# Experts of a routed feed-forward layer: 71 tiles in place of 72, with the last turns of the loops written out

## The reference

```
def _L1_ffn_ref(x, router_w, w_gate, w_up, w_down):   # x: 4096 tokens of 128, 8 experts, hidden 512, top 2
    scores = jax.nn.softmax(xf @ router_w.T, axis=-1)
    topk_scores, topk_ids = jax.lax.top_k(scores, TOP_K)
    topk_scores = topk_scores / topk_scores.sum(-1, keepdims=True)
    cw = (jax.nn.one_hot(topk_ids, N_EXPERTS, dtype=xf.dtype) * topk_scores[..., None]).sum(1)
    def body(acc, inputs):
        wg, wu, wd, w = inputs
        h = jax.nn.silu(xf @ wg) * (xf @ wu)
        return (acc + w[:, None] * (h @ wd), None)
# in the whole: x = x + 0.5 * _L1_ffn_ref(_layernorm(x), ...)
```

## Time and profile before

| | |
|---|---|
| median of three runs | 1526.19 us (1525.87 to 1528.49) |
| the profiled execution | 1528.99 us |
| its span, first to last instruction | 1527.3 us |
| mean granted TensorE clock | 0.876 |
| busy: PE, DVE, ACT, POOL | 76%, 65%, 52%, 39% of the span |
| instructions on all engines | 34396 |
| the first routed layer's tiles | about 680 to 886 us |
| the second routed layer's tiles | about 1290 to 1497 us |

### The profile page before, as it was taken

How to read it: one execution, slowest core, us unless ns; L and a number is a source line. 1 busy time by engine, 2 the same in 40 slices (tenths; PEclk the granted TensorE clock), 3 DMA queues, 4 the chain that set the end, 5 groups by cost and what they waited for, 6 DMA issues and landing times.

```text
span 1527.3 us, 34396 instructions
## 1 busy us (share of the span) xinstructions
PE 1166.0 (76%) x11393; PEld 901.6 (59%) x11394; DVE 997.7 (65%) x1974; ACT 787.2 (52%) x1333; POOL 592.1 (39%) x859
## 2 busy tenths in 40 slices
PE   0577559999984776549999914899998654999991
PEld 0355336666652555539999912455554353999991
DVE  5799769898955998573333356888997357333333
ACT  0444216555663443236666661567666523666666
POOL 2122122121200222016676723566766301667671
PEclk9999659999997998559999966899999855999996
DMA  8000023322210000101111133343243010111115
GB/s 255 19 1 0 1 49 58 53 55 55 51 24 1 1 0 1 55 9 46 47 48 46 47 123 56 58 78 65 56 83 58 2 56 9 46 47 48 47 47 178
DMA packets 161960, 75.58 MB, mean 49 GB/s; under 512 B 126540, under 2 KB 153941, under 8 KB 161877
## 3 DMA queue, kind: packets, MB, share of 16 engines
q1 hardware_dynamic: 152404, 55.06, 16.4%
q0 software_dynamic: 9472, 19.42, 4.3%
HBM read 28.69 MB, written 15.86 MB: 29 GB/s over the span
## 4 chain that ended last, share of the span: by engine, by line
PE 53%; DVE 24%; issue 7%; ACT 6%; DMA 3%; POOL 3%; SPq 2%; DVEq 1%; POOLq 0%; ACTq 0%
PE PS L990 17%; PE PS L1010 8%; PE PS L656 4%; PE PS L358 3%; DVE sg L790 2%; PE PS L638 2%; PE PS L622 2%; PE PS L575 2%; DVE m L790 2%; PE PS L950 2%; PE PS L610 1%; ACT pt L1070 1%; SPq L882 1%; DVE q_amax L266 1%; DMA qT<-qs 1%
## 5 line engine op out<-in xcount | busy, mean ns | idle before, releaser
L990 PE MATMUL PS<-xTs,pt 128*128 128x128 f32 x2336 | 287.7, 277 | 0.0
L715 ACT ACTIVATE pt<-PS 128x768 f32<-128x768 f32 (+1 forms) x256 | 227.6, 917 | 111.2 <-PE PS L638 59.4
L990 PEld LDWEIGHTS PS<-xTs,pt 128*128 128x128 f32 x2336 | 276.0, 194 | 0.0
L1114 DVE TENSOR_TENSOR pt<-pt,PS 128x512 f32<-128x512 f32 x146 | 100.4, 687 | 240.4 <-PE PS L990 210.9
L1227 POOL DMA_INDIRECT xs<-rows,src x152 | 147.3, 969 | 193.3 <-DVE src L1108 147.6
L1039 ACT ACTIVATE pt<-wgu 128x1024 f32 x148 | 156.2, 1057 | 93.2 <-issue 84.2
L1236 POOL DMA_INDIRECT outs<-ys,dst x144 | 142.0, 986 | 85.6 <-DVE ys L1122 78.5
L790 DVE TENSOR_REDUCE m<-PS 128x4 f32<-128x1024 f32 x128 | 149.2, 1217 | 12.9 <-PE PS L575 12.3
L1010 PE MATMUL PS<-wdn,pt 128*128 x1152 | 152.2, 275 | 0.0
L1010 PEld LDWEIGHTS PS<-wdn,pt 128*128 128x128 f32 x1152 | 140.0, 192 | 0.0
L575 PE MATMUL PS<-tables 64*128 64x128 bf16 (+2 forms) x1536 | 132.0, 251 | 0.0
(11 more groups left out here) (228 smaller groups left out, 2120.2 us busy)
## 6 DMA issues: line engine op xcount, KB each, us to landing
pt<-outs SPq DMA_DIRECT2D x16, 512.0 KB, 5.0
rows<-qT SPq DMA_DIRECT2D x12, 256.0 KB, 2.4
xs<-rows,src POOLq DMA_INDIRECT x152, 2.5
outs<-ys,dst POOLq DMA_INDIRECT x144, 2.3
wgu<-in_L_ffn_w_gate SPq DMA_DIRECT2D x1, 2048.0 KB
wgu<-in_L_ffn_w_up SPq DMA_DIRECT2D x1, 2048.0 KB
wdn<-in_L_ffn_w_down SPq DMA_DIRECT2D x8, 256.0 KB
qT<-hqT SPq DMA_DIRECT2D x128, 4.0 KB
```

Of the source, the lines that this page charges most:

```text
L715: s.activation(k.pt[:, a % 4, :, 0:w], k.PS[:, self.bank:self.bank + 2, 0:w], ACT.Exp, scale=self.scale).then_inc(self.s_p, 1)
L990: last = t.matmul(k.PS[:, 1 + 2 * p + w, c * P:(c + 1) * P], k.wst[:, 1 - p, w, c * P:(c + 1) * P], k.xTs[:, p, :], start=True, stop=True)
L1114: v.tensor_tensor(k.hs[:, p, :], k.sgs[:, p, :], k.PS[:, 2 + 2 * p, :], ALU.mult).then_inc(self.s_h, 1)
```

## The change

NS is 71, NL equals NS, and nothing is prepared for tiles beyond the last. Since 71 is divisible by neither 24 nor 4, the bodies of PE's, ACT's and DVE's loops became functions `tiles(m)`: with a loop variable they write a whole body, with a Python number they write only the tiles that exist (`has`). PE's loop now has 2 passes (48 tiles), and 23 tiles stand written out behind it. ACT's loop has 17 passes, with what is left of tiles 69 and 70 behind it. DVE's loop also ends after tile 67, with three tiles behind it. POOL gathers 71 times. The semaphores' final counts now differ over the four ring buffers (`self.turns`, `self.t0`).

```diff
@@ -42,11 +42,11 @@
 GT = 4
 NG = NT // GT
 RING = 4
-NS = 72
+NS = 71
 UN = 24
 TABLES = P + 2 * P + 3 * 384
-NL = NS + RING
-assert NS % UN == 0 and UN % RING == 0 and NS >= (2 * NT * P + NE * (P - 1)) // P
+NL = NS
+assert UN % RING == 0 and NS >= (2 * NT * P + NE * (P - 1)) // P
 CR = 2
 ROUND = 1.5 * 2.0 ** 23
 
@@ -926,7 +926,8 @@
         self.s_stored = k.sem(name + "_stored")
         self.s_scaled = k.sem(name + "_scaled")
 
-        self.ld0, self.st0 = run * 16 * (NS // RING + 1), run * 16 * (NS // RING)
+        self.turns = [len(range(u, NS, RING)) for u in range(RING)]
+        self.t0 = [run * 16 * n for n in self.turns]
         self.ga0 = run * 16 * (NG // RING)
         self.s_ld = [k.sem(f"moe_loaded_{i}") for i in range(RING)]
         self.s_st = [k.sem(f"moe_stored_{i}") for i in range(RING)]
@@ -974,7 +975,7 @@
             return t.value_load(k.eid[0:1, ds(n, 1)], min_val=0, max_val=NE - 1)
 
         def xT(n, r, before, back):
-            eng.wait_ge(self.s_ld[r], self.ld0 + 16 * before + 16)
+            eng.wait_ge(self.s_ld[r], self.t0[r] + 16 * before + 16)
             if back:
                 eng.wait_ge(self.s_xT, n - 1)
             t.transpose(k.PS[:, 7 * (r % 2), 0:P], k.xs[:, r, 0:D], k.ident[:, :]).then_inc(self.s_xT_ps, 1)
@@ -996,14 +997,22 @@
         xT(1, 1, 0, False)
         up(0, 0, 0)
         up(0, 0, 1)
-        with eng.Fori(0, NS // UN) as m:
+
+        def has(n):
+            return not isinstance(n, int) or n < NS
+
+        def tiles(m):
             e = expert(UN * m)
             for u in range(UN):
                 i, p = UN * m + u, u % 2
-                up(i + 1, 1 - p, 0)
-                up(i + 1, 1 - p, 1)
-                xT(i + 2, (u + 2) % RING, UN // RING * m + (u + 2) // RING, True)
-                e1 = expert(i + 1) if u + 1 < UN else None
+                if not has(i):
+                    break
+                if has(i + 1):
+                    up(i + 1, 1 - p, 0)
+                    up(i + 1, 1 - p, 1)
+                if has(i + 2):
+                    xT(i + 2, (u + 2) % RING, UN // RING * m + (u + 2) // RING, True)
+                e1 = expert(i + 1) if u + 1 < UN and has(i + 1) else None
                 eng.wait_ge(self.s_h, i + 1 + CR)
                 eng.wait_ge(self.s_y, i + CR)
                 for c in range(FC):
@@ -1011,6 +1020,9 @@
                                     start=c == 0, stop=c == FC - 1)
                 last.then_inc(self.s_y_ps, 1)
                 e = e1
+        with eng.Fori(0, NS // UN) as m:
+            tiles(m)
+        tiles(NS // UN)
 
     def scalar(self, eng):
         k, s = self.k, self.k.nc.scalar
@@ -1055,12 +1067,22 @@
         xT(0, 0, False)
         xT(1, 1, False)
         silu(0, 0)
-        with eng.Fori(0, NS // RING) as m:
+
+        def has(n):
+            return not isinstance(n, int) or n < NS
+
+        def tiles(m):
             for u in range(RING):
                 i, p = RING * m + u, u % 2
-                weights(i + 2, p, True)
-                silu(i + 1, 1 - p)
-                xT(i + 2, p, True)
+                if has(i + 2):
+                    weights(i + 2, p, True)
+                if has(i + 1):
+                    silu(i + 1, 1 - p)
+                if has(i + 2):
+                    xT(i + 2, p, True)
+        with eng.Fori(0, NS // RING) as m:
+            tiles(m)
+        tiles(NS // RING)
 
         for g in range(NG):
             eng.wait_ge(self.s_ga[g % RING], self.ga0 + 16 * (g // RING) + 16)
@@ -1112,18 +1134,26 @@
             eng.wait_ge(self.s_up_ps, n + 1)
             eng.wait_ge(self.s_y_ps, n - 1 + CR)
             v.tensor_tensor(k.hs[:, p, :], k.sgs[:, p, :], k.PS[:, 2 + 2 * p, :], ALU.mult).then_inc(self.s_h, 1)
+
+        def has(n):
+            return not isinstance(n, int) or n < NS
+
         def tiles(m):
             for u in range(RING):
                 i, p = RING * m + u, u % 2
-                h(i + 1, 1 - p)
+                if not has(i):
+                    break
+                if has(i + 1):
+                    h(i + 1, 1 - p)
                 eng.wait_ge(self.s_y_ps, i + 1 + CR)
-                if not isinstance(m, int) or self.run:
-                    eng.wait_ge(self.s_st[u], self.st0 + 16 * m)
+                if not isinstance(m, int) or m or self.run:
+                    eng.wait_ge(self.s_st[u], self.t0[u] + 16 * m)
                 v.tensor_copy(k.ys[:, u, :], k.PS[:, 6, 0:D]).then_inc(self.s_y, 1)
         h(0, 0)
         tiles(0)
         with eng.Fori(1, NS // RING) as m:
             tiles(m)
+        tiles(NS // RING)
 
         for g in range(NG):
             eng.wait_ge(self.s_scaled, g + 1)
@@ -1218,7 +1248,7 @@
         k, g = self.k, self.k.nc.gpsimd
         for u in range(RING):
             if self.run:
-                eng.wait_ge(self.s_ld[u], self.ld0)
+                eng.wait_ge(self.s_ld[u], self.t0[u])
         eng.wait_ge(k.sem("pad_rows_stored"), 32)
         eng.wait_ge(self.s_stored, 16 * NG)
         eng.wait_ge(self.s_list, 1)
@@ -1231,7 +1261,8 @@
         for i in range(NS):
             u = i % RING
             eng.wait_ge(self.s_xT_ps, i + 1)
-            gather(i + RING)
+            if i + RING < NS:
+                gather(i + RING)
             eng.wait_ge(self.s_y, i + 1 + CR)
             g.indirect_dma_start(k.outs, bass.IndirectOffsetOnAxis(ap=k.dst[:, i:i + 1], axis=0),
                                  k.ys[:, u, :], None).then_inc(self.s_st[u], 16)
@@ -1243,9 +1274,9 @@
             sp.dma_start(k.rows[2 * P + g * GT * P:2 * P + (g + 1) * GT * P, :].rearrange("(j p) d -> p j d", p=P),
                          k.xng[g]).then_inc(self.s_stored, 16)
         for u in range(RING):
-            sp.wait_ge(self.s_st[u], self.st0 + 16 * (NS // RING))
-        sp.wait_ge(self.s_h, NS + 1 + CR)
-        sp.wait_ge(self.s_wst, NS + 2)
+            sp.wait_ge(self.s_st[u], self.t0[u] + 16 * self.turns[u])
+        sp.wait_ge(self.s_h, NS + CR)
+        sp.wait_ge(self.s_wst, NS)
         def put(g):
             if self.last:
                 sp.dma_start(out[g * GT * P:(g + 1) * GT * P, :].rearrange("(t p) d -> p t d", p=P),
@@ -1264,7 +1295,7 @@
             sp.wait_ge(self.s_added, g + 1)
             put(g)
         for u in range(RING):
-            sp.wait_ge(self.s_ld[u], self.ld0 + 16 * (NS // RING) + 16)
+            sp.wait_ge(self.s_ld[u], self.t0[u] + 16 * self.turns[u])
 
 
 class Core:
```

## The result

The changed kernel takes 1519.5 us (five executions, 1517.7 to 1521.1), the kernel before beside it 1526.8. The ratio is 0.9949, with a 95% interval of 0.9939 to 0.9960: 0.5% faster, inside the forecast range and 3 us above the forecast. The same kernel measured again in another set came to 1517.5 us and a ratio of 0.9940 (0.9924 to 0.9956). The change is worth 7 to 10 us.

The account below looks back on a forecast made before the run. PE was taken to set the pace of the tiles, DVE that of the lists. 4.15 + 0.71 = 4.86 us a layer, 9.7 in both, off 1526.19 gave 1516.5 us, range 1514.5 to 1518.5 (80 in 100).

Parts of the forecast that it names:

- Tiles: End of each layer's tiles: 4.69 us of PE's work go, 0.54 come back as a wait; gain 4.15 us a layer.
- The wait for one bank: Last down product on PE waits for DVE's copy of the tile before, as both use one bank: 0.54 us back.
- the 0.05 us from DVE's end to PE's load: At the last down product: PE's first weight load was taken to start 0.05 us after DVE's copy ends.
- The scatter: POOL's last scatter follows DVE's copy by 0.29 us, as before; the gather ahead of it was not counted as a cost.
- Lists: List stage ahead of the tiles, bound by DVE: narrower tables save 0.71 us a layer.
- Straight code and the ways out of the loops: PE's written-out tiles and ACT's and DVE's loop exits cost 0; rival that late instruction fetches stop PE: 1544 us, 3 in 100.
- The slack of ACT and DVE: At their loops' ends: ACT's weight copy ends 1.13 us before PE needs it, so leaving the loops stays hidden.
- The start: First 32 `up` matmuls at half clock: half of the 0.71 us gained ahead may be lost, 0.35 a layer, 1517.2 us.
- a fixed moment: Start of the tiles: the clock may rise at the same moment as before, not as long after the start; 0.35 a layer.
- The rival in which the look-ahead is worth nothing: End of the tiles: the 1.9 us of `up(72)` and `xT(73)` come back whole; 1519.2 us, 9 in 100.

Follow-up runs that it names:

- the kernel with the clock raised beforehand: The changed kernel with eleven matmuls of ident by ident on PE between the lists and the first tile: 1511.4 us.

## Why the prediction was right

**Tiles.** Right in mechanism and nearly in size: 3.96 us a layer in place of 4.15. A tile is 2.79 us to the second digit (72 tiles against 71). The wait for one bank came as named. It cost 0.73 and not 0.54; the step that erred is the 0.05 us from DVE's end to PE's load, of which 0.10 is the second wait.

**The scatter.** This step failed in size, and it is the largest part of what was missing that the change itself is shown to cause. The prediction had the last scatter follow the copy by 0.29 us, because it did in every tile. It didn't see that removing the gather moves the gather's wait onto the scatter. The start came 0.46 us later, in each layer; 0.37 are left at the load of the results. The code, with its waits, showed beforehand that it moves; what it costs no row of before could tell.

**Lists.** 0.70 us a layer, 0.71 forecast. Straight code and the ways out of the loops: 0 forecast and 0 seen. The slack of ACT and DVE was enough.

**The start.** The prediction's sum left it at 0 and kept 0.35 a layer as what may come back; 0.23 and 0.52 came back in the stretch. That the tiles start at half rate and pay some 2 us a layer for it is shown by the kernel with the clock raised beforehand. That the earlier start is what made it dearer is not: with untouched lists the second layer's stretch took 11.49 us in one profile and 11.92 in another. The premise, a fixed moment, is wrong as a rule, as PE's own work ahead moves it.

Taking the stretches, 9.7 less 0.4 (tiles), 0.75 (scatter) and 0.75 (start) is 7.8 us, or 8.6 without the start, and the two sets measured 7.3 and 9.5. The sum is confirmed by the stretches and not by the times: with 3 us that come and go between the layers, a time inside the range is partly luck. The rival in which the look-ahead is worth nothing had the nearest time, 1519.2 us, but not the cause: 1.17 of the 1.9 us that it wrote off did come at the copy, and 0.8 are left at the load.

## What to carry to other kernels

When an instruction is removed, look where its wait goes: a condition that was already met can, as a second wait, still delay the next instruction, here by 0.47 us. Where a pipeline drains, nothing covers the hand-overs any more, so each removed look-ahead gives back part of its own time. And if PE stands idle ahead of its densest stage at the lower clock, matmuls without a purpose can pay nearly as much as a tile that is left out: 2.0 to 2.3 us a layer against 2.79.

## What the runs showed of the hardware

An indirect DMA behind one wait starts 0.28 us after the awaited copy ends, behind two waits 0.75 us, though the other had long been met. For PE, one wait less before its weight load was worth 0.1 us.

Some 4.6 us of matmuls in a pause raised the clock for the stage behind it: 3.75 us against 4.9 to 6.2 for the same 32 matmuls. And the clock's steps fall differently from profile to profile: one stage that nobody touched took 42.2 us in one and 39.1 in another, and the stretch between the layers 372 or 375. Differences of 3 us between single profiles of this kernel are therefore not evidence by themselves; stretches with equal clock are.
